# The second tile of the second attention: its norms by ScalarE, its q normed first on VectorE

## The reference, cut to what matters

```python
q, k, v = jnp.split(h @ wqkv, 3, axis=-1)            # 8 heads of 64
q = l2norm(q) * qs;  k = l2norm(k) * ksc             # t / clip(norm(t), 1e-12)
q, k = rotary_xpos(q, k)
o = local_attention(q, k, v)                         # windows of 64, softmax over 128 keys
x = x + o @ wo
```

## Time and profile before

| | us |
|---|---|
| median of 3 runs | 548.8 (548.55 to 549.55) |
| the profiled execution, its own time | 549.87 |
| its span in the trace | 548.1 |
| its mean granted TensorE clock | 0.958 of full |
| TensorE busy | 494.0 (90%) |
| VectorE busy | 427.0 (78%) |
| ScalarE busy | 349.6 (64%) |
| GpSimd busy | 339.3 (62%) |

### The profile page before, as it was taken

One profiled execution on the slowest core, in us unless ns is written; L12 is line 12 of the kernel. 1 busy time (PEld: TensorE's weight loads), 2 busy tenths in 40 slices (PEclk: granted clock), 3 DMA queues, 4 the chain that ended last, 5 costly groups with the idle time before them and its releaser, 6 DMA issues.

```text
span 548.1 us, 11812 instructions
## 1 busy us (share of the span) xinstructions
PE 494.0 (90%) x4059; PEld 315.8 (58%) x4059; DVE 427.0 (78%) x1173; ACT 349.6 (64%) x1001; POOL 339.3 (62%) x271
## 2 busy tenths in 40 slices
PE   5844088999999999999899999999999999999996
PEld 5424033567777776443467777777544445667775
DVE  6999999899888976566889988995545687566665
ACT  5854007699999987534679999998556526533332
POOL 5990028999999998668989999994111277410000
PEclk9975579999999999999989999999999999999999
DMA  8600003211111112000221111111000000000000
GB/s 300 238 1 1 0 3 109 56 39 32 40 40 41 41 39 71 0 2 0 77 49 35 37 41 39 41 40 31 1 1 0 0 1 1 1 1 19 22 20 19
DMA packets 15025, 20.98 MB, mean 38 GB/s; under 512 B 2379, under 2 KB 9013, under 8 KB 14709
## 3 DMA queue, kind: packets, MB, share of 16 engines
q1 hardware_dynamic: 14676, 20.13, 13.3%
q10 hardware_dynamic: 288, 0.08, 0.1%
HBM read 9.99 MB, written 1.05 MB: 20 GB/s over the span
## 4 chain that ended last, share of the span: by engine, by line
PE 68%; DVE 18%; POOL 6%; issue 4%; ACT 3%; DMA 1%; DVEq 0%; SPq 0%; POOLq 0%; ACTq 0%
PE psT L1523 11%; PE psQK L1615 9%; PE psO L1738 6%; PE psO L1670 5%; PE psQK L1945 5%; PE psS L1718 5%; DVE vst L1108 3%; DVE vAB L1112 3%; PE psO L1523 3%; PE psS L2017 3%; PE psQK L1752 3%; PE psO L2017 2%; PE psQK L1877 2%; PE psS L1854 2%; PE psQK L1756 2%
## 5 line engine op out<-in xcount | busy, mean ns | idle before, releaser
L576 ACT ACTIVATE prob<-psS,nmx 128x128 f32<-128x128 f32 x256 | 90.1, 378 | 18.2 <-DVE nmx L1248 18.2
L904 POOL TENSOR_TENSOR rn<-ssq,half 128x16 f32<-128x16 f32 x32 | 93.2, 2913 | 8.6 <-DVE ssq L1234 8.5
L896 POOL TENSOR_TENSOR ra<-ra,rb 128x512 f32<-128x512 f32 x64 | 81.0, 1286 | 1.0 <-DVE rb L1216 0.8
L716 POOL TENSOR_TENSOR rst<-mv,half 128x4 f32<-128x4 f32 x24 | 25.7, 1072 | 73.8 <-DVE mv L1009 64.2
L1615 PE MATMUL psQK<-wqkv,hsA 128*128 128x512 f32 x128 | 62.0, 604 | 1.0 <-DVE hsA L1197 0.6
L576 ACT ACTIVATION_READ_ACCUMULATOR prob<-psS,nmx 128x1 f32 x256 | 55.4, 216 | 0.0
L912 POOL TENSOR_TENSOR qkn<-ra,rn 128x512 f32<-128x512 f32 x32 | 49.0, 1532 | 2.5
L1213 DVE TENSOR_TENSOR ra<-psQK,rope 128x512 f32<-128x512 f32 x64 | 43.9, 686 | 7.5 <-PE psQK L1615 6.6
L1216 DVE TENSOR_TENSOR rb<-psQK,rope 128x512 f32<-128x512 f32 x64 | 43.5, 680 | 0.0
L697 ACT ACTIVATE gel<-psQK 128x512 f32<-128x512 f32 x32 | 19.1, 597 | 37.5 <-PE psQK L1945 37.5
L1227 DVE TENSOR_REDUCE ssq<-sq 128x8 f32<-128x512 f32 x64 | 41.1, 676 | 1.6 <-ACT sq L516 1.3
(11 more groups left out here) (263 smaller groups left out, 1177.6 us busy)
## 6 DMA issues: line engine op xcount, KB each, us to landing
vAB<-vAB SPq DMA_DIRECT2D x62, 128.0 KB, 2.2
wqkv<-in_wqkv SPq DMA_DIRECT2D x2, 768.0 KB, 8.2
big<-in_x SPq DMA_DIRECT2D x4, 256.0 KB, 5.3
ra<-in_rope_t SPq DMA_DIRECT2D x1, 1024.0 KB, 7.7
ropeb<-in_rope SPq DMA_DIRECT2D x1, 1024.0 KB, 8.6
big<-in_ew SPq DMA_DIRECT2D x2, 512.0 KB, 4.1
wmod<-in_wmod SPq DMA_DIRECT2D x2, 384.0 KB, 6.8
out<-big SPq DMA_DIRECT2D x3, 256.0 KB, 2.3
```

The costliest lines, as they stand in the source:

```text
L576: act.activation(prob[:, k, :], psS[:, hb, c * P:(c + 1) * P], ACT.Exp, bias=nmx[:, k:k + 1], accum_out=sums[:, n % 2, k:k + 1]).then_inc( ...
L896: pool.tensor_tensor(o, o, rb[:, r], ALU.add).then_inc(s["sum_" + name], 1)
L904: pool.tensor_tensor(rn[:, :], ssq[:, :], half[:, :], ALU.pow).then_inc(s["rn_ready"], 1)
```

## The change

ScalarE gets a `norms` of its own, which computes ssq to the power -0.5 as the exponential of -0.5 times the logarithm. It is used for tile 17 only, behind the copies of tile 16; GpSimd skips `norms` for that tile. VectorE norms q of tile 17 at the head of its call with i = -1 in the second layer, ahead of the k rope products of tile 18 and of the two negmax of tile 16. Ahead of the second attention the table set that has both the logarithm and the exponential is asked for.

```diff
@@ scalar
+            def power(dst, src):
+                own.one(act.activation(dst, src, ACT.Ln, bias=0.0, scale=1.0))
+                return act.activation(dst, dst, ACT.Exp, bias=0.0, scale=-0.5)
+
+            def norms(n):
+                act.wait_ge(s["ssq_max"], n + 1)
+                if n:
+                    act.wait_ge(s["k_ready"], n)
+                    act.wait_ge(s["q_ready"], n)
+                power(rn[:, :], ssq[:, :]).then_inc(s["rn_ready"], 1)
...
                     k_turned(n + 2)
                     if n != 1 - LEAD:
                         v_copy(n + 2)
+                    if n == NT + 1 - LEAD:
+                        norms(NT + 1)
...
                 if l == 0:
                     act.wait_ge(s["table"], 3)
+                    act.preload_act_table_set("natural_log_exp_and_others")
                     load_table(ACT.Exp)
@@ gpsimd
                 if has(i + 2):
-                    norms(n + 2)
+                    if n + 2 != NT + 1:
+                        norms(n + 2)
                     k_normed(n + 2)
@@ vector
                 if i == 2 - LEAD:
+                    if l:
+                        q_normed(n + 2)
                     rope_products(n + 3, 1)
                     negmax(n + 1, 0)
                     negmax(n + 1, 1)
-                    if l:
-                        q_normed(n + 2)
                     rope_products(n + 3, 0)
```

## The result

| | before | after |
|---|---|---|
| median, 15 runs each, us | 548.71 (548.55 to 550.6) | 551.2 (549.79 to 552.38) |
| ratio of the two | | 1.0038, 95% interval 1.0031 to 1.0046 |
| span of the profiled execution, us | 548.1 | 549.5 |
| GpSimd busy, us | 339.3 | 335.6 |

The change made the kernel slower, by 2.5 us on the medians and by 0.38% (2.1 us) on the ratio, where no measurable change and a range of 548.0 to 550.1 were forecast. The shape of the stall came out as drawn; two of its terms did not.

What follows compares the result with a forecast made beforehand. TensorE's ring in the second attention was taken to bound the kernel. Its start, the turned output of tile 16, moves from 283.44 to 282.55, so 549.87 - 0.9 = 549.0, against a median of 548.8; range 548.0 to 550.1.

Steps and rivals of the forecast that it cites:

- The shape of the stall: TensorE's 1.88 us idle before tile 17's q turn becomes 2.35 us before tile 19's q projection, awaiting tile 18's q squares.
- The start of the second attention sets the end: Second attention is a ring of TensorE work, 7.27 us per tile; moving its start moves the kernel's end equally.
- the pair: ScalarE's 128x16 logarithm and exponential for the norms of tile 17, taken as 0.44 us together.
- port and clock as forecast: VectorE norms q of tile 17 in 0.69 us and the clock stays up: 0.3 us later than before.
- The median of before: The 548.8 median probably stands for executions without the clock's fall at the second attention's start; the sum gave 548.65.
- so VectorE should win if it is free: Both engines wait for tile 17's norms; VectorE was to start first, its q norm taking 0.69 and GpSimd's k norm 1.55.
- a k norm of 1.04 on GpSimd: Sign that the prediction is wrong: GpSimd's k norm takes 1.04 us, its price where GpSimd started first, instead of 1.55.
- the rival: GpSimd gets the shared SBUF port first at tile 17, q norm costs 0.9 us more: 549.9, chance 0.07.
- the clock's fall: TensorE's clock falls behind its idle time in most changed executions and few of before: about 1.05 us, 550.0, chance 0.08.
- The rivals: Start gained in full 546.8 (0.11), GpSimd first 549.9 (0.07), clock fall in most 550.0 (0.08), something unseen (0.04).

Runs made afterwards that it cites:

- experiment 6: Changed kernel plus GpSimd's k norm of tile 17 waiting for VectorE's q norm, and eight unread TensorE products before tile 19's q projection; 548.99, ratio 1.0.
- experiment 4: Changed kernel with eight unread products on TensorE between the k and q projection of tile 19, to hold the clock; 549.96, ratio 1.0019.
- the three kernels with the port lost: Changed kernel (551.2), and it with VectorE's q norm awaiting the norms last (551.3) or with two of four waits moved ahead of the residual (551.1).
- experiment 3: Changed kernel with one more wait: GpSimd's k norm of tile 17 waits for VectorE's q norm of tile 17; 550.11, ratio 1.0016.
- experiment 1: Changed kernel with VectorE's old order: ScalarE norms tile 17, q is normed behind the rope products and both negmax; 548.26, ratio 0.9984.
- the norms awaited last: Changed kernel with VectorE's q norm of tile 17 waiting for the norms last instead of first, same waits otherwise; 551.3.
- experiment 5: Kernel before with seven unread products on TensorE ahead of the q and k turns of tile 17; 548.65, ratio 0.9997.
- experiment 7: Kernel before with one more wait: GpSimd's k norm of tile 17 waits for VectorE's q norm of tile 17; 548.71, ratio 0.9995.
- experiments 11 and 12: Changed kernel with VectorE's old order and ScalarE also norming tile 18: 548.15; the same with GpSimd's rope sums of tile 19 behind tile 18's q norm: 547.57.
- two waits: Changed kernel with two of the four waits of VectorE's q norm of tile 17 moved ahead of the residual before it; 551.1.
- one wait: Changed kernel with two q norm waits moved ahead of the residual and the residual's own wait dropped, leaving only the norms' wait; 549.5.

## Why the prediction was wrong

**What held.** The start of the second attention sets the end: 1.43 us there, 1.4 in the span. ScalarE's norms were ready at 269.30 (forecast 269.4), and the pair took 0.49 (0.44). The stall did move from the q turn to the q projection of tile 19, released by the q squares. The change with port and clock as forecast was to cost 0.3 us over a kernel before with the clock up, and experiment 6 measured 0.3 (548.99 against 548.66). The median of before does stand for executions without the fall there: taking the fall away did not move it (548.65).

**The step that failed: "so VectorE should win if it is free".** The forecast took VectorE's 0.69 for the q norm because VectorE had started 0.05 ahead of GpSimd in the steady part, and because GpSimd's release by ScalarE took 0.08. I took for granted that VectorE's own release would again be 0.03. It was 0.08, of which 0.04 is the semaphore instruction between the norms and the q norm (L1258). The order puts the q norm right behind the residual, whose wait makes a fourth; in the steady part it has three, and VectorE started 0.03 us behind the norms (284.28 + 2.91 to 287.22). The prediction had named a k norm of 1.04 on GpSimd as a sign that it is wrong, and that is what the trace shows. GpSimd's timeline of the kernel before, for the 284.28:

```profile
284.28 2.91 POOL L904 TENSOR_TENSOR rn<-ssq,half 128x16 f32<-128x16 f32 x1 [1.22 <-DVE ssq L1234]
```

The condition that I gave for the rival (norms before 269.15) was wrong as well: the port was lost with VectorE idle for 0.25 us. The rival's mechanism and its price stood there (0.9 more, 549.9), but with a chance of 0.07. Measured, the price is 0.90 in the trace and 549.96 - 548.99 = 0.97 on the medians.

**The second: the clock's fall was priced rightly and given too small a chance.** I gave it 1.05 us and a chance of 0.08 for most executions. Judged by the times it is there in most: eleven of fifteen runs are at 551.09 or more, and experiment 4 takes them all away. The idle time was 0.75 and 2.29 us rather than 2.35 in one. The lost port makes the fall more frequent but is not all of it: by their times 20 of the 25 runs of the three kernels with the port lost had it, and still six of eleven in experiment 3, where the port was not lost. The price is 551.2 - 549.96 = 1.24 in the changed kernel. About 0.9 of it is there when the projection of tile 20 starts (284.54 against 283.54 with the clock held, less 0.12 by which the q norm started later), for which the forecast had 1.05. The other 0.3 is a second loss of the port: VectorE's q norm of tile 19 took 1.56 there, GpSimd having started 0.03 ahead (287.81 against 287.84), and TensorE waited for the turned output of tile 17; with the clock held it did not (the projections of tiles 20 and 21 start at 283.54 and 290.82 there, 7.28 apart, against 7.60 in the changed kernel).

The rivals were summed as if only one could happen, and here two happened at once. The account in full, on the medians: 548.66 before, + 0.33 for the order net of ScalarE's gain, + 0.97 for the port, + 1.24 for the clock, is 551.2. Each term is the difference of two medians in a row, so that they add up is no proof; what speaks for them is that each was taken away by an edit of its own. Split further by experiment 1, ScalarE's norms gain 0.4 and the order costs 0.7 before port and clock.

**Left open.** What sets the clock's fall in some executions of a kernel and not in others, and how long it lasts (in the profiled execution with the norms awaited last, 552.4, the lower level held for 6.8 us), the 0.5 to 0.8 us in four runs of experiment 5, and how a wait comes to be a semaphore instruction of its own.

## What to carry to other kernels

Before putting an instruction ahead of others, list what is then queued behind it: here a q norm that nobody needed for another 2 us held up the exponentials that everybody needed. Where two engines that compete for the port wait for the same semaphore, do not reckon with the price of one order of starting. Make the order explicit, with the engine whose work is on the path first, or count the dearer price. Look then at what the engine that now goes second is late with: in experiment 7 that took the gain back. An early result paid here only once no unneeded work of the other engine was in its way (experiments 11 and 12). And after moving a stall, ask whether the clock falls behind the idle time that it leaves on TensorE, since that comes on top and not instead.

## What the runs showed of the hardware

- Whether VectorE started 0.03 us behind GpSimd or 0.04 ahead of it moved the kernel's median by 1.6 us (551.1 with two waits, 549.5 with one), 0.8 to 0.9 of it in executions whose clock stayed up.
- VectorE's q norm started 0.03 us behind its release, with one wait and in the steady part with three, and 0.08 to 0.13 where a semaphore instruction stood between. So the place of that instruction counts, not the number of waits.
- Idle times of 1.88, and of 0.75 and 2.29 us on TensorE were followed in some executions by the lower of its two clock levels, for about 3.4 us and once for 6.8 us; in other executions the same idle times were not (with two waits, 549.72, the granted clock stayed at 1.00). Eight bf16 products in the second of them, 1.89 us, prevented it in all eleven runs, by their times (0.57 us of idle time left).
- A clamp of 128x16 on VectorE, 0.17 us, took 0.71 beside a GpSimd sum of 128x512, and ended with it, so the price is not in proportion to the instruction that is held up.
